# Row maxima of the attention layer: penalties subtracted on TensorE, a plain maximum over two units at a time on VectorE

## The chip, the cores and the metric

The kernel runs on one core of a Trainium2 chip. The metric is the device time of one execution of the whole program, in microseconds (us). The trace is that of one profiled execution.

## What is computed

The program runs four graph layers over 12500 nodes and 200000 edges, each followed by a layer normalisation. The change lies in the last one, an attention layer over the edges taken in both directions and a loop at every node:

```python
src = jnp.concatenate([src0, dst0, loop])
dst = jnp.concatenate([dst0, src0, loop])
xt = x @ W
s_node = xt @ a_src
d_node = xt @ a_dst
e_all = jnp.concatenate([e_contrib, e_contrib, zeros])
logits = leaky_relu(s_node[src] + d_node[dst] + e_all, 0.2)
m = segment_max(logits, dst)
z = exp(logits - m[dst])
out = segment_sum((z / segment_sum(z, dst)[dst])[:, None] * xt[src], dst)
```

The stage that the change touches finds, for each node, the largest `s_node[src] + e_all` over its edges (`d_node[dst]` is the same for all edges of a node and the leaky relu keeps the order, so both are put on afterwards).

## The kernel before

Edges lie in slots: a **group** `g` is 128 chunks (one per partition) of four edges (`SLOTS`), all of a group's edges ending in the same block of 128 nodes. There are 544 groups for each of the two directions `k`. A **unit** is one group of one direction: 128 × 4 = 512 edges. `QUAD` = 4 groups of both directions are handled together, so a **quad** is eight units, and there are 136 quads. The loop `skewed` runs `RING` = 4 quads to an iteration, 34 iterations, and lets stages run a quad or two ahead of one another.

The stage is the function `attention_maxima`. What each engine does for a quad:

- SyncE (`load`, L2007 and L2011) fetches the rows of direction 1 and, for both directions, the edges' node keys, broadcast to all partitions (512 KB each). The rows wait for the scores of two quads before, the keys for the penalties of two quads before.
- GpSimd (`gather`, L2046) fetches the rows of direction 0 with four indirect DMAs, and (`split`, L2032 to L2038) splits the 32 scores of each partition into three bf16 parts.
- VectorE (`scores`, L2114 and L2115) makes those scores, two quads ahead of the maxima.
- TensorE (`turn`, L2089) transposes the parts to `gT` (96 × 128), one quad ahead, and (`spread`, L2098) writes, for each unit, its 512 scores into all 128 partitions of one PSUM bank `wide[v]`, with four matmuls of 128 columns. The stationary operand `pick` selects one row of each part; nothing is accumulated.
- ScalarE (`copy_turned` L2078, `keep` L2065, `penalties` L2072) copies `gT` out of PSUM, keeps the scores, and makes for each direction `pen` = |key − partition| · 2^100 over 2048 edges: zero where the edge ends in the node of that partition, huge elsewhere.
- VectorE (`maxima`, L2127) makes, for each unit, one fused instruction that subtracts `pen` from `wide` and takes the maximum into one column of `gm`, followed by the read of its accumulator; then eight small maxima (L2136) of those columns into the blocks' entries of `tops`. At the head of each loop iteration it loads the iteration's block numbers into registers (`blocks`, L2140).

The order around the change is set by counted semaphores. TensorE's unit `e` may be written when the unit that last lay in its bank has been reduced; there are four banks, so TensorE runs up to four units ahead:

```python
wait(pe, s_max, q * 2 * QUAD + k * QUAD + v - QUAD + 1)
for r in range(SLOTS):
    m = nc.tensor.matmul(wide[v][:, r, :], pick[...], gT[:, u % 2, :], start=True, stop=True)
```

VectorE waits for `s_pen` (ScalarE's penalties) and `s_w` (TensorE's unit); ScalarE's penalties of quad `q` wait for `s_max` of quad `q - 2`, whose `pen` they overwrite.

Of the kernel before, what the change touches and what calls it, by code (L numbers as in the profile page):

```python
# [5 lines left out]
F32 = mybir.dt.float32  # L6
BF16 = mybir.dt.bfloat16
ALU = mybir.AluOpType
ACT = mybir.ActivationFunctionType
AX = mybir.AxisListType  # L10
# [4 lines left out]
P = 128  # L15
# [4 lines left out]
SLOTS = 4  # L20
# [723 lines left out]
def finished(*added):  # L744

    for s, n in added:
        s.base += n


def wait(eng, s, value):  # L750

    if isinstance(value, int) and value <= 0:
        return
    if isinstance(s, Count):
        eng.wait_ge(s.sem, value + s.base)
    else:
        eng.wait_ge(s, value)
# [1207 lines left out]

QUAD = 4
AHEAD = 3
FAR = 2.0 ** 100


def attention_maxima(nc, counts, D, K, name, XB, YB, score, tops):
# [6 lines left out]
    with ExitStack() as ctx:  # L1978
        def sb(nm, s, d=F32):
            return ctx.enter_context(nc.sbuf_tensor(f"{name}_{nm}", s, d))  # L1980
        keys = [sb(f"keys{k}", [P, 2, QUAD, SLOTS * P], BF16) for k in range(2)]
        pen = [sb(f"pen{k}", [P, 2, QUAD, SLOTS * P], BF16) for k in range(2)]
# [3 lines left out]
        gp = sb("gp", [P, 2, 3, NQ], BF16)  # L1986
        gT = sb("gT", [3 * NQ, 2, P], BF16)
        pick = sb("pick", [3 * NQ, NQ, P], BF16)
        junk = sb("junk", [P, 2, SLOTS * P], BF16)
        gm = sb("gm", [P, 2, 2 * QUAD])  # L1990
        far = sb("far", [P, 1])
        tp = [ctx.enter_context(nc.psum_tensor(f"{name}_t{u}", [3 * NQ, P], BF16)) for u in range(2)]
        wide = [ctx.enter_context(nc.psum_tensor(f"{name}_wide{u}", [P, SLOTS, P], F32)) for u in range(QUAD)]
        s_key = [[counts.get(f"expand_keys_loaded{k}{u}") for u in range(2)] for k in range(2)]
        s_in = [[counts.get(f"sum_rows_in{k}{u}", k == 0) for u in range(2)] for k in range(2)]
        s_pick, s_far = counts.get("top_pickers"), counts.get("top_far")
# [3 lines left out]
        with nc.Block() as block:  # L2000
            @block.sync
            def _(sp):
                def load(i, u):
                    q = i * RING + u
                    w = u % 2
                    wait(sp, s_g, q - 1)
                    sp.dma_start(rows[1][:, w, :, :, :].rearrange("p v r c -> p v (r c)"), view[:, bass.ds(q * QUAD, QUAD), :]).then_inc(s_in[1][w].sem, 16)  # L2007
                    for k, kr in enumerate((K.krA, K.krB)):
                        at = kr[0:1, 0:1]
                        wait(sp, s_pen, 2 * (q - 1))  # L2010
                        sp.dma_start(keys[k][:, w, :, :].rearrange("p v e -> p (v e)"),  # L2011
                                     bass.AP(tensor=at.tensor, offset=at.offset + q * (QUAD * SLOTS * P), ap=[[0, P], [1, QUAD * SLOTS * P]])).then_inc(s_key[k][w].sem, 16)
                skewed(sp, n, [(1, load)])
# [42 lines left out]

            @block.scalar
            def _(act):
                nc.scalar.activation(far[:, :], K.iotac[:, :], ACT.Copy, scale=-FAR).then_inc(s_far.sem, 1)
                wait(act, s_far, 1)  # L2060

                def keep(i, u):
                    q = i * RING + u
                    wait(act, s_g, q + 1)
                    nc.scalar.copy(score[:, :, bass.ds(q * QUAD, QUAD), :], g4[:, u % 2, :, :, :]).then_inc(s_kept.sem, 1)  # L2065

                def penalties(i, u):
                    q = i * RING + u
                    for k in range(2):
                        wait(act, s_key[k][u % 2], (i * (RING // 2) + u // 2 + 1) * 16)  # L2070
                        wait(act, s_max, (q - 1) * 2 * QUAD)
                        nc.scalar.activation(pen[k][:, u % 2, :, :], keys[k][:, u % 2, :, :], ACT.Abs, bias=far[:, :], scale=FAR).then_inc(s_pen.sem, 1)  # L2072

                def copy_turned(i, u):
                    q = i * RING + u
                    wait(act, s_t, q + 1)
                    wait(act, s_w, (q - 1) * 2 * QUAD)
                    nc.scalar.copy(gT[:, u % 2, :], tp[u % 2][:, :]).then_inc(s_tc.sem, 1)  # L2078
                skewed(act, n, [(1, copy_turned), (1, keep), (1, penalties)])

            @block.tensor
            def _(pe):
                wait(pe, s_pick, 6)

                def turn(i, u):
                    q = i * RING + u
                    wait(pe, s_gp, q + 1)
                    wait(pe, s_tc, q - 1)
                    nc.tensor.transpose(tp[u % 2][:, :], gp[:, u % 2, :, :].rearrange("p a e -> p (a e)"), K.identb[:, :]).then_inc(s_t.sem, 1)  # L2089

                def spread(i, u):
                    q = i * RING + u
                    wait(pe, s_tc, q + 1)
                    for k in range(2):
                        for v in range(QUAD):
                            wait(pe, s_max, q * 2 * QUAD + k * QUAD + v - QUAD + 1)
                            for r in range(SLOTS):
                                m = nc.tensor.matmul(wide[v][:, r, :], pick[:, (k * QUAD + v) * SLOTS + r, :], gT[:, u % 2, :], start=True, stop=True)  # L2098
                            m.then_inc(s_w.sem, 1)
                skewed(pe, n, [(1, turn), (0, spread)])  # L2100

            @block.vector
            def _(dve):
                held = {}

                def scores(i, u):
                    q = i * RING + u
                    w = u % 2
                    for k in range(2):
                        need = (i * (RING // 2) + u // 2 + 1) * 16  # L2110
                        wait(dve, s_in[k][w], need * QUAD if k == 0 else need)
                    wait(dve, s_kept, q - 1)
                    wait(dve, s_gp, q - 1)
                    nc.vector.tensor_tensor(g4[:, w, 0, :, :], rows[0][:, w, :, :, C], K.ecA[:, bass.ds(q * QUAD, QUAD), :], ALU.add)  # L2114
                    nc.vector.tensor_copy(g4[:, w, 1, :, :], rows[1][:, w, :, :, C]).then_inc(s_g.sem, 1)  # L2115

                def maxima(i, u):
                    q = i * RING + u
                    w = u % 2
                    for k in range(2):  # L2120
                        wait(dve, s_pen, 2 * q + k + 1)
                        for v in range(QUAD):
                            e = k * QUAD + v
                            wait(dve, s_w, q * 2 * QUAD + e + 1)
                            wait(dve, s_max, q * 2 * QUAD + e - 1)
                            dve.nop(nofuse=True)
                            nc.vector.tensor_tensor_reduce(out=junk[:, e % 2, :], in0=wide[v][:, :, :].rearrange("p r e -> p (r e)"),  # L2127
                                                           in1=pen[k][:, w, v, :], scale=1.0, scalar=-FAR, op0=ALU.subtract, op1=ALU.max,
                                                           accum_out=gm[:, w, e:e + 1]).then_inc(s_max.sem, 1)
                    wait(dve, s_max, (q + 1) * 2 * QUAD)  # L2130
                    for v in range(QUAD):
                        for k in range(2):
                            b = held[k][u * QUAD + v]
                            top, e = tops[2 * (v % 2) + k], k * QUAD + v
                            wait(dve, s_top, q * 2 * QUAD + 2 * v + k - 3)
                            nc.vector.tensor_tensor(top[:, bass.ds(b, 1)], top[:, bass.ds(b, 1)], gm[:, w, e:e + 1], ALU.max).then_inc(s_top.sem, 1)  # L2136

                def blocks(i):
                    for k in range(2):
                        held[k] = nc.values_load_multi_w_load_instructions(K.cblk[0:1, k, bass.ds(i * RING * QUAD, RING * QUAD)], engines=DVE_ONLY,  # L2140
                                                                           min_val=0, max_val=D.blocks - 1, skip_runtime_bounds_check_because=CLAMPED)[1]
                skewed(dve, n, [(2, scores), (0, maxima)], blocks)
        NQs = D.NG // QUAD
        for k in range(2):
            finished(*[(s, 8 * NQs) for s in s_key[k]], *[(s, (QUAD if k == 0 else 1) * 8 * NQs) for s in s_in[k]])
        finished((s_pick, 6), (s_far, 1), (s_g, NQs), (s_kept, NQs), (s_gp, NQs), (s_t, NQs), (s_tc, NQs), (s_pen, 2 * NQs),
                 (s_w, 2 * D.NG), (s_max, 2 * D.NG), (s_top, 2 * D.NG), (s_r, 3 * NQs))


def attention_sums(nc, counts, D, K, name, XB, YB, score, M3, accT):  # L2150
# [585 lines left out]
```

## Time and profile before

| | us |
|---|---|
| median of 3 runs | 16084.6 (16077.82 to 16091.67) |
| the profiled execution | 16079.79 |
| its span in the trace | 16078.1 |
| first fused maximum (L2127) starts | 13492.8 |
| last fused maximum (L2127) starts | 14563.0 |

The first two rows are device times; the span is that of the trace, and 1.7 us of the profiled execution lie outside of it. The two last rows bound the stage that the change touches: 1070.2 us, or 6.7% of the span. Over the whole span TensorE is busy 64% and VectorE 63%.

### The profile page before, as it was taken

The numbers are of one execution on the slowest core, as the hardware profiler recorded it, in microseconds if no ns is written. First come the engines' busy times: TensorE is split into PE (matmuls) and PEld (weight loads), VectorE is DVE, ScalarE is ACT, GpSimd is POOL, SyncE is SP. The second block draws the span as 40 slices with busy tenths as digits, with TensorE's granted clock in tenths as the row PEclk, the third lists the DMA queues.
The fourth block names the chain that finished last, engine by engine and source line by source line (L and its number), as shares of the span: only waits on it lengthen the run. The fifth ranks groups of instructions, "written<-read, shape, count | busy, mean of one in ns | idle before, by whom it ended". The sixth has DMA issues, their size and how long they took to land. (4 is left out here: it accounts for less than half of the span.)

```text
span 16078.1 us, 333902 instructions
## 1 busy us (share of the span) xinstructions
PE 10302.2 (64%) x72558; PEld 7980.5 (50%) x72559; DVE 10167.2 (63%) x36116; ACT 4495.2 (28%) x11901; POOL 9058.1 (56%) x10038
## 2 busy tenths in 40 slices
PE   6555555555537777767965656645566776667886
PEld 5333333333326666656853444422344664336886
DVE  9666666666643444437856777752365666887887
ACT  0111111111102333322113430025301223556886
POOL 0477777777745777767764445546400555554442
PEclk9777777777766777765556667755555665557998
DMA  9722222222242444453319997756653897885665
GB/s 369 303 80 79 81 81 79 79 83 79 79 94 58 80 80 80 80 79 71 68 28 279 324 309 223 224 163 218 191 176 89 279 278 257 270 267 204 212 212 160
DMA packets 2144346, 2589.93 MB, mean 161 GB/s; under 512 B 892242, under 2 KB 1761819, under 8 KB 2144195
## 3 DMA queue, kind: packets, MB, share of 16 engines
q1 hardware_dynamic: 1749158, 1741.66, 37.6%
q0 software_dynamic: 353792, 655.17, 13.1%
q10 hardware_dynamic: 41244, 191.56, 3.1%
q14 instruction: 115, 0.93, 0.0%
q8 instruction: 37, 0.61, 0.0%
HBM read 1738.44 MB, written 848.86 MB: 161 GB/s over the span
## 5 line engine op out<-in xcount | busy, mean ns | idle before, releaser
L566 POOL DMA_INDIRECT edges_by_dst<-rec,pos x1568 | 1541.2, 983 | 1029.1 <-DVE rec L501 555.5
L989 POOL DMA_INDIRECT sc_rows<-src_table,sc_idx x1664 | 1589.1, 955 | 607.9 <-issue 497.6
L566 POOL DMA_INDIRECT edges_by_cell<-rec,pos x1568 | 1545.5, 986 | 514.8 <-issue 497.4
L1756 PE MATMUL ex_rows<-table,ex_oh 128*128 x6528 | 1132.6, 339 | 884.8 <-DVE ex_stage L1732 335.7
L1844 PE MATMUL gs_part<-gs_rows,gs_oh 128*128 128x192 bf16 x6528 | 1024.4, 321 | 602.0 <-DVE gs_oh L1817 518.5
L1756 PEld LDWEIGHTS ex_rows<-table,ex_oh 128*128 128x128 bf16 x6528 | 724.9, 129 | 1292.3 <-issue 1252.6
L642 PE MATMUL xps<-ident,ea 128*128 128x128 f32 x784 | 216.4, 431 | 1740.9 <-DMA ea<-in_edge_attr_dram 1740.9
L1844 PEld LDWEIGHTS gs_part<-gs_rows,gs_oh 128*128 128x128 bf16 x6528 | 697.0, 131 | 929.3 <-issue 613.5
L2224 ACT ACTIVATE key_in_block<-at_rows,first_node 128x66 f32<-128x66 f32 x4352 | 1083.3, 336 | 266.2 <-PE at_part L2252 244.9
L2252 PE MATMUL at_part<-cell_edge_term,key_in_block 128*66 128x128 f32 x8704 | 1062.7, 286 | 115.3 <-issue 96.4
L530 DVE SCALAR_TENSOR_TENSOR junk<-rowb,keycol,earlier 128x128 f32<-128x128 f32 (+1 forms) x3136 | 1124.5, 415 | 1.8
L1724 DVE TENSOR_SCALAR ex_oh<-ex_keys,iotac 128x512 bf16<-128x512 bf16 x1632 | 568.2, 359 | 840.4 <-PE ex_rows L1756 628.1
L2252 PEld LDWEIGHTS at_part<-cell_edge_term,key_in_block 128*66 128x66 f32 x8704 | 1020.1, 146 | 137.4 <-issue 125.7
L642 PEld LDWEIGHTS xps<-ident,ea 128*128 128x128 f32 x784 | 139.5, 216 | 1818.7 <-issue 1818.6
L2204 POOL DMA_INDIRECT at_rows<-scored_rows_by_src,chunk_read_by_src x544 | 564.3, 1037 | 801.8 <-ACT key_in_block L2224 664.5
L635 PE MATMUL look<-Csb,ohT 128*128 128x256 f32 x3136 | 974.4, 441 | 0.7 <-DVE junk L543 0.7
L1951 PE MATMUL ex_rows<-table,ex_oh 128*128 x13056 | 783.9, 227 | 263.8 <-DVE own_terms L1924 144.3
L2098 PE MATMUL mx_wide<-mx_gT,mx_pick 96*128 96x128 bf16 x4352 | 653.9, 307 | 411.3 <-DVE mx_gm L2127 408.5
L1707 POOL DMA_INDIRECT dst_rows_by_src<-ex_stage,chunk_by_src x544 | 527.0, 969 | 632.7 <-DVE ex_stage L1732 508.6
L592 ACT COPY eaT<-xps 128x512 f32<-128x512 f32 x196 | 114.9, 586 | 2714.0 <-PE xps L642 2714.0
L1951 PEld LDWEIGHTS ex_rows<-table,ex_oh 128*128 128x128 bf16 x13056 | 700.5, 118 | 347.2 <-issue 307.3
L520 DVE TENSOR_TENSOR prod<-ea,a 128x128 f32<-128x128 f32 x196 | 58.1, 296 | 1280.1 <-DMA ea<-in_edge_attr_dram 1280.1
(402 smaller groups left out, 27327.5 us busy)
## 6 DMA issues: line engine op xcount, KB each, us to landing
ex_keys<-src_key_rows SPq DMA_DIRECT2D x1632, 128.0 KB
gs_rows<-dst_rows_by_src SPq DMA_DIRECT2D x1088, 192.0 KB
rowb<-sort_key_rows SPq DMA_DIRECT2D x392, 512.0 KB, 5.2
ex_keys<-dst_key_rows SPq DMA_DIRECT2D x1088, 128.0 KB
dst_rows_by_src<-patY ACTq DMA_DIRECT2D x1, 104448.0 KB, 417.2
rows_by_src<-ex_stage SPq DMA_DIRECT2D x544, 192.0 KB
scored_dst_rows_by_src<-patZ ACTq DMA_DIRECT2D x1, 71808.0 KB, 637.9
scored_rows_by_src<-ex_stage SPq DMA_DIRECT2D x544, 132.0 KB
```

The costliest lines, as they stand in the source:

```text
L530: nc.vector.scalar_tensor_tensor(junk[:, j % 4, k, 1 - odd:2, :], rowb[:, u, k, j - odd:j + 1, :], keycol[:, u, 1 - k, j:j + 1], earlier[: ...
L566: nc.gpsimd.indirect_dma_start(out=out, out_offset=bass.IndirectOffsetOnAxis(ap=pos[:, u, k, j:j + 1], axis=0), in_=row, in_offset=None).t ...
L635: m = nc.tensor.matmul(look[(u * PAIRS + c) % LOOKS][:, j % 2, :, :], ohT[:, u, j, :], Csb[:, c % 4, :, :], start=True, stop=True)
L989: nc.gpsimd.indirect_dma_start(out=rows[:, u, j, :], out_offset=None, in_=tabS, in_offset=bass.IndirectOffsetOnAxis(ap=idx[:, u, j:j + 1], ...
L1724: nc.vector.tensor_scalar(oh[k][:, u % 2, :], keys[k][:, u, :], K.iotac[:, :], None, ALU.is_equal).then_inc(s_oh[k].sem, 1)
L1756: m = nc.tensor.matmul(rows[k][u % 2][r // 2][:, r % 2, 0:W], oh[k][:, u % 2, r * P:(r + 1) * P], t3[:, bass.ds(held[k][u], 1), :].rearran ...
L1844: m = nc.tensor.matmul(part[k][u][:, 0, :], oh[k][:, u % 2, :, r], rows[k][:, u, r, :], start=r == 0, stop=r == SLOTS - 1)
L1951: m = nc.tensor.matmul(rows[k][u % 2][:, r, :], oh[k][:, u % 2, r * P:(r + 1) * P], t3[:, bass.ds(held[k][u], 1), part * W:(part + 1) * W] ...
L2098: m = nc.tensor.matmul(wide[v][:, r, :], pick[:, (k * QUAD + v) * SLOTS + r, :], gT[:, u % 2, :], start=True, stop=True)
L2204: nc.gpsimd.indirect_dma_start(out=rows[0][:, q % 2, v, :, :].rearrange("p r c -> p (r c)"), out_offset=None, in_=XB, in_offset=bass.Indir ...
L2224: m = nc.scalar.activation(msg[:, e % RING, r, :], rows[k][:, u % 2, v, r, :], ACT.Copy, scale=z[:, u % 2, k, v, r:r + 1])
L2252: m = nc.tensor.matmul(part[e % RING][:, 0, :], msg[:, e % RING, r, :], oh[:, e % RING, r, :], start=r == 0, stop=r == SLOTS - 1)
```

## The change

The subtraction moves from VectorE to TensorE. ScalarE makes once a constant `minus`, the negated identity (bf16). For each unit TensorE first multiplies it with that unit's 512 penalties, which writes their negative into the bank (`start=True`), and the four matmuls of `spread` now accumulate onto that (`start=False`). What lies in PSUM is then score minus penalty, and VectorE needs only a plain `tensor_reduce` with the maximum. It takes two units (two banks, 1024 elements, two results) at a time. The four banks are now two buffers of two banks (`WIDE` = 2) in place of four of one. `junk` goes away.

The waits follow. TensorE waits for the penalties (`s_pen`) itself, and for the reduction of the pair before last. ScalarE's penalties wait for TensorE's `s_w` in place of VectorE's `s_max`. `s_w` and `s_max` count pairs.

```diff
+WIDE = 2
...
-        junk = sb("junk", [P, 2, SLOTS * P], BF16)
+        minus = sb("minus", [P, P], BF16)
...
-        wide = [ctx.enter_context(nc.psum_tensor(f"{name}_wide{u}", [P, SLOTS, P], F32)) for u in range(QUAD)]
+        wide = [ctx.enter_context(nc.psum_tensor(f"{name}_wide{u}", [P, 2, SLOTS, P], F32)) for u in range(WIDE)]
...
+                nc.scalar.activation(minus[:, :], K.identb[:, :], ACT.Copy, scale=-1.0).then_inc(s_far.sem, 1)
                 nc.scalar.activation(far[:, :], K.iotac[:, :], ACT.Copy, scale=-FAR).then_inc(s_far.sem, 1)
-                wait(act, s_far, 1)
+                wait(act, s_far, 2)
...
-                        wait(act, s_max, (q - 1) * 2 * QUAD)
+                        wait(act, s_w, (q - 1) * QUAD)
                         nc.scalar.activation(pen[k][:, u % 2, :, :], keys[k][:, u % 2, :, :], ACT.Abs, bias=far[:, :], scale=FAR).then_inc(s_pen.sem, 1)
...
-                    wait(act, s_w, (q - 1) * 2 * QUAD)
+                    wait(act, s_w, (q - 1) * QUAD)
...
                     for k in range(2):
-                        for v in range(QUAD):
-                            wait(pe, s_max, q * 2 * QUAD + k * QUAD + v - QUAD + 1)
-                            for r in range(SLOTS):
-                                m = nc.tensor.matmul(wide[v][:, r, :], pick[:, (k * QUAD + v) * SLOTS + r, :], gT[:, u % 2, :], start=True, stop=True)
+                        wait(pe, s_pen, 2 * q + k + 1)
+                        for h in range(QUAD // 2):
+                            e = k * (QUAD // 2) + h
+                            wait(pe, s_max, q * QUAD + e - WIDE + 1)
+                            for v in (2 * h, 2 * h + 1):
+                                to = wide[e % WIDE][:, v % 2, :, :]
+                                nc.tensor.matmul(to.rearrange("p r e -> p (r e)"), minus[:, :], pen[k][:, u % 2, v, :], start=True, stop=False)
+                                for r in range(SLOTS):
+                                    m = nc.tensor.matmul(to[:, r, :], pick[:, (k * QUAD + v) * SLOTS + r, :], gT[:, u % 2, :],
+                                                         start=False, stop=r == SLOTS - 1)
                             m.then_inc(s_w.sem, 1)
...
-                    for k in range(2):
-                        wait(dve, s_pen, 2 * q + k + 1)
-                        for v in range(QUAD):
-                            e = k * QUAD + v
-                            wait(dve, s_w, q * 2 * QUAD + e + 1)
-                            wait(dve, s_max, q * 2 * QUAD + e - 1)
-                            dve.nop(nofuse=True)
-                            nc.vector.tensor_tensor_reduce(out=junk[:, e % 2, :], in0=wide[v][:, :, :].rearrange("p r e -> p (r e)"),
-                                                           in1=pen[k][:, w, v, :], scale=1.0, scalar=-FAR, op0=ALU.subtract, op1=ALU.max,
-                                                           accum_out=gm[:, w, e:e + 1]).then_inc(s_max.sem, 1)
-                    wait(dve, s_max, (q + 1) * 2 * QUAD)
+                    for e in range(QUAD):
+                        wait(dve, s_w, q * QUAD + e + 1)
+                        dve.nop(nofuse=True)
+                        nc.vector.tensor_reduce(gm[:, w, 2 * e:2 * e + 2], wide[e % WIDE][:, :, :, :].rearrange("p v r e -> p v (r e)"),
+                                                AX.X, ALU.max).then_inc(s_max.sem, 1)
+                    wait(dve, s_max, (q + 1) * QUAD)
```

How this stands on the two engines, in the first loop iteration. On VectorE the eight fused maxima of a quad, each with the read of its accumulator, stand before the eight small maxima; of those 16 rows the first six:

```order
L2127 ISA mx_junk,mx_gm<-mx_wide,mx_pen 128x512
L2127 ISA mx_gm 128x1
L2127 ISA mx_junk,mx_gm<-mx_wide,mx_pen 128x512
L2127 ISA mx_gm 128x1
L2127 ISA mx_junk,mx_gm<-mx_wide,mx_pen 128x512
L2127 ISA mx_gm 128x1
```

In their place the changed kernel has, for a whole quad, between the scores and the small maxima:

```order
L2123 TENSOR_TENSOR mx_g<-mx_rows,cell_edge_term 128x16
L2124 COPY mx_g<-mx_rows 128x16
L2132 TENSOR_REDUCE mx_gm<-mx_wide 128x2 x4
L2140 ISA
L2140 TENSOR_TENSOR tops<-tops,mx_gm 128x1
```

Sixteen instructions became four.

On TensorE a quad was a transpose and 32 matmuls of 128 columns:

```order
L2089 MATMUL mx_t<-identb,mx_gp 96x128
L2098 MATMUL mx_wide<-mx_gT,mx_pick 128x128 x32
```

In the changed kernel it is the same with a matmul of 512 columns ahead of each four, eight times in a quad; its first two pairs of units:

```order
L2092 MATMUL mx_t<-identb,mx_gp 96x128
L2104 MATMUL mx_wide<-mx_pen,mx_minus 128x512
L2106 MATMUL mx_wide<-mx_gT,mx_pick 128x128 x4
L2104 MATMUL mx_wide<-mx_pen,mx_minus 128x512
L2106 MATMUL mx_wide<-mx_gT,mx_pick 128x128 x4
L2104 MATMUL mx_wide<-mx_pen,mx_minus 128x512
L2106 MATMUL mx_wide<-mx_gT,mx_pick 128x128 x4
L2104 MATMUL mx_wide<-mx_pen,mx_minus 128x512
L2106 MATMUL mx_wide<-mx_gT,mx_pick 128x128 x4
```

The columns that TensorE streams for a unit went from 512 to 1024, and they stand in one queue with no other work between.

## Rows read from the trace of the kernel before

**Rows 1.** Busy time by stretch: the changed stage, then three stages with bf16 or fp32 matmuls.

```profile
core 0: us, PE busy (x) PEld busy (x) DVE busy (x) ACT busy (x) POOL busy (x), PEclk, DMA share, GB/s
13493.00:14563.00 1070.00, 659.23 (x4470) 394.50 (x4470) 872.52 (x3519) 578.16 (x537) 626.09 (x1066) 0.50 0.81 265
12450.00:13400.00 950.00, 715.98 (x11924) 639.27 (x11920) 586.05 (x2489) 218.82 (x994) 482.57 (x498) 0.69 0.90 279
9700.00:10500.00 800.00, 514.48 (x3637) 379.40 (x3636) 596.30 (x1816) 0.00 (x0) 455.27 (x455) 0.78 0.74 224
14600.00:15900.00 1300.00, 1153.83 (x12373) 1106.21 (x12374) 1093.12 (x2577) 1044.04 (x4260) 527.40 (x513) 0.93 0.62 212
```

**Rows 2.** Groups of instructions in the stage: busy us, mean ns, idle before and releaser.

```profile
L2127 DVE CUSTOM_DVE_ANT_0 mx_junk<-mx_wide,mx_pen 128x512 bf16<-128x512 f32 x1088 | 675.8, 687 | 25.0 <-ACT mx_pen L2072 18.2 <-issue 6.2
L2098 PE MATMUL mx_wide<-mx_gT,mx_pick 96*128 96x128 bf16 x4352 | 653.9, 307 | 411.3 <-DVE mx_gm L2127 408.5
L2072 ACT ACTIVATE mx_pen<-mx_keys,mx_far 128x2048 bf16<-128x2048 bf16 x272 | 529.5, 1994 | 158.1 <-DVE mx_gm L2127 158.1
L2136 DVE TENSOR_TENSOR tops<-tops,mx_gm 128x1 f32 x1088 | 161.7, 160 | 38.4 <-DVE mx_gm L2127 28.7 <-DVE tops L2136 0.3
```

**Rows 3.** Who waited for whom in the stage: us in total, times, longest us.

```profile
PEld mx_wide L2098 <- DVE mx_gm L2127: 650.5, 911, 5.6
POOL mx_gp L2032 <- DVE mx_g L2115: 207.4, 122, 5.5
DVE mx_g L2114 <- issue: 134.1, 129, 3.3
```

**Rows 4.** Instructions in order of time, one quad from 13999.43 to the next.

```profile
13999.43 0.69 DVE L2127 CUSTOM_DVE_ANT_0 mx_junk<-mx_wide,mx_pen 128x512 bf16<-128x512 f32 x1 [0.20 <-issue]
14000.05 0.08 DVE L2127 DVE_READ_ACCUMULATOR2_ANT mx_gm<- 128x1 f32 x1
14000.05 0.69 DVE L2127 CUSTOM_DVE_ANT_0 mx_junk<-mx_wide,mx_pen 128x512 bf16<-128x512 f32 x1
...
14000.66 0.08 DVE L2127 DVE_READ_ACCUMULATOR2_ANT mx_gm<- 128x1 f32 x1
14000.66 0.69 DVE L2127 CUSTOM_DVE_ANT_0 mx_junk<-mx_wide,mx_pen 128x512 bf16<-128x512 f32 x1
14000.80 0.34 PEld L2098 LDWEIGHTS mx_wide<-mx_gT,mx_pick 96*128 96x128 bf16 x4 [0.27 <-DVE mx_gm L2127]
...
14002.42 0.31 PE L2089 MATMUL mx_t<-identb,mx_gp 128*96 128x128 bf16 x1
...
14002.87 0.26 ACT L2078 COPY mx_gT<-mx_t 96x128 bf16<-96x128 bf16 x1 [4.58 <-PE mx_t L2089]
...
14004.33 0.08 DVE L2127 DVE_READ_ACCUMULATOR2_ANT mx_gm<- 128x1 f32 x1
...
14004.63 1.26 DVE L2136 TENSOR_TENSOR tops<-tops,mx_gm 128x1 f32 x8 [0.22 <-DVE mx_gm L2127]
...
14006.13 0.18 DVE L2114 TENSOR_TENSOR mx_g<-mx_rows,cell_edge_term 128x16 f32<-128x16 f32 x1 [0.24 <-issue]
...
14006.56 0.69 DVE L2127 CUSTOM_DVE_ANT_0 mx_junk<-mx_wide,mx_pen 128x512 bf16<-128x512 f32 x1 [0.16 <-ACT mx_pen L2072]
```

**Rows 5.** The same view at the loop's head: VectorE's stop while it loads block numbers.

```profile
14030.75 0.18 DVE L2114 TENSOR_TENSOR mx_g<-mx_rows,cell_edge_term 128x16 f32<-128x16 f32 x1 [3.22 <-issue]
```

**Rows 6.** The same view at the stage's start: 16 spread matmuls with nothing to wait for.

```profile
13489.44 1.91 PE L2098 MATMUL mx_wide<-mx_gT,mx_pick 96*128 96x128 bf16 x16
```

**Rows 7.** Groups of the whole span: TENSOR_REDUCE on VectorE at three sizes.

```profile
L1103 DVE TENSOR_REDUCE scores<-sc_qk 128x256 f32 x408 | 168.3, 412 | 0.0
L1290 DVE TENSOR_REDUCE sm_edge<-sm_pen 128x1 f32<-128x1664 f32 x2 | 3.8, 1886 | 0.1
L884 DVE TENSOR_REDUCE ln_m<-x_nodes 128x104 f32<-128x6656 f32 x4 | 28.3, 7086 | 1.7 <-PEq L2421 1.1 <-PEq L788 0.6
```

**Rows 8.** The only bf16 matmul of 512 columns in the trace.

```profile
L614 PE MATMUL xps<-zero 128*128 128x512 bf16 x1 | 0.6, 586 | 2.9 <-PEq L352 2.9
```

More of the change, by code:

```diff
@@ L2083, in _ @@
                 wait(pe, s_pick, 6)
+                wait(pe, s_far, 2)
                 def turn(i, u):
@@ L2145, in attention_maxima @@
             finished(*[(s, 8 * NQs) for s in s_key[k]], *[(s, (QUAD if k == 0 else 1) * 8 * NQs) for s in s_in[k]])
-        finished((s_pick, 6), (s_far, 1), (s_g, NQs), (s_kept, NQs), (s_gp, NQs), (s_t, NQs), (s_tc, NQs), (s_pen, 2 * NQs),
-                 (s_w, 2 * D.NG), (s_max, 2 * D.NG), (s_top, 2 * D.NG), (s_r, 3 * NQs))
+        finished((s_pick, 6), (s_far, 2), (s_g, NQs), (s_kept, NQs), (s_gp, NQs), (s_t, NQs), (s_tc, NQs), (s_pen, 2 * NQs),
+                 (s_w, D.NG), (s_max, D.NG), (s_top, 2 * D.NG), (s_r, 3 * NQs))
 def attention_sums(nc, counts, D, K, name, XB, YB, score, M3, accT):
```

## The prediction

> **What bounds the stage now.** I read the busy time by stretch first [rows 1]. In the changed stage VectorE is busy 872 of 1070 us, TensorE 659, ScalarE 578, GpSimd 626, the DMA engines 0.81. Nothing is full, so the waits decide. They say [rows 3] that TensorE waits for VectorE's maxima (650 us), GpSimd for VectorE's scores (207 us), and VectorE for "issue", its own registers and branches (134 us). VectorE is the pace. The order of time shows a quad in full [rows 4]: the fused maxima start 0.61 us apart (13999.43, 14000.05, 14000.66), the last accumulator read ends at 14004.41, 4.98 us after the start, then come 0.22 us, eight small maxima (1.26 us), 0.24 us, the scores, and the next quad at 14006.56. A quad is **7.13 us: 4.98 us of maxima and 2.15 us of tail.** Every fourth quad has a stop of 3.22 us in place of 0.24 [rows 5]; 136 × 7.13 + 34 × 2.98 = 1071 us, the stage's 1070. TensorE hides: it needs about 0.43 us for a unit against VectorE's 0.61, and four banks let it run ahead. Its clock was granted at 0.50 throughout (1.2 GHz) [rows 1].
>
> **VectorE's part.** Eight fused maxima go, four TENSOR_REDUCE of 1024 elements come. The rows for that operation [rows 7] are 412 ns at 256, 1886 ns at 1664, 7086 ns at 6656, thus 1.042 ns an element and 0.15 us fixed; 1024 elements give 1886 − 640 × 1.042 = **1.22 us**. The fused one lasts 0.687 us and starts every 0.612 [rows 2, 4], so 0.075 us of it overlaps the next; I give the reduce the same, a pitch of **1.144 us**. If VectorE alone decided, a quad's maxima would last 3 × 1.144 + 1.22 = 4.65 us in place of 4.98: 0.33 us less, 45 us over 136 quads. That is all there is to gain; two fused units cost 1.225 us, one pair 1.144. The Trainium skill (VectorE: DVE Perf Modes, "The DRAIN you can't avoid") speaks against even that: it says that the next operation does not start until the pipe is empty, and grants an earlier start only to one that isn't held. By its first half the reduces would start 1.22 us apart, and the sum below, in its full-rate quads, would be some 6 us higher; the fused rows overlap, so I keep 1.144.
>
> **TensorE's part.** Sixteen matmuls back to back took 1.91 us [rows 6]; less one matmul's length beyond its pitch (0.314 − 0.107) that is 0.107 us per 128 columns at 1.2 GHz. The added matmul has 512 columns, so 0.427 us. The one such row of the trace [rows 8] is 586 ns long against 314 for 128 columns, 0.27 more for 384 columns, which would make it 0.38; I take 0.427, since back-to-back pitch is what counts here. Weight loads overlap, as they do now. A pair of units costs 2 × (0.427 + 4 × 0.107) = **1.71 us at half rate**, half of that, **0.85 us, at full rate** (2.4 GHz). A quad needs 6.8 us or 3.4 us of TensorE.
>
> **The hand-over is the point.** There are now two buffers, each a pair. TensorE may fill a buffer only when its reduce is over, and VectorE may read only when it is full. From [rows 4]: accumulator read over at 14000.74, weight load at 14000.80, so 0.06 us that way; transpose over at 14002.73, ScalarE's copy at 14002.87, so 0.14 us the other way. Let a quad's first reduce start at 0 with both buffers full (TensorE had the 2.15 us tail for that).
>
> - Half rate: reduce 0 ends at 1.22, TensorE fills from 1.28 to 2.99, its last matmul's result is there at 3.20, reduce 2 starts at 3.34 instead of 2.29. The second fill follows directly: its result at 4.91, reduce 3 starts at 5.05 and ends at 6.27. Against 4.98 now: **+1.29 us**, with a quad of 8.42 us, of which TensorE works 6.9.
> - Full rate (the same 0.21 us beyond the pitch): reduce 2 starts at 2.48; the other buffer is free at 2.42, reduce 3 starts at 3.62 and ends at 4.84: **−0.14 us**.
>
> So all quads at half rate would give +175 us, all at full rate −19 us.
>
> **Which rate.** The stage now streams 512 columns a unit in short bursts and is granted 0.50. It will stream 1024, at half rate nearly without a break inside a quad. The stages in which TensorE works in long bursts with stops are granted 0.69 and 0.78, the one that hardly stops 0.93 [rows 1]. Here a full-rate quad leaves TensorE idle for half of it, and each iteration has the stop of [rows 5], so I take the stretches with stops as the nearest: full rate 0.38 and 0.56 of the time, half rate 0.62 and 0.44. I put **half of the quads at half rate**: 0.5 × 1.29 − 0.5 × 0.14 = 0.575 us a quad, × 136 = **+78 us**; the two ends, 0.44 and 0.62, give +67 and +102.
>
> **The rest at nothing.** ScalarE's penalties (2 × 1.99 us [rows 2]) now start when TensorE has read those of two quads before, earlier in the cycle than now; with the two copies ScalarE has 4.5 us of work in a quad of 7 or more. TensorE's new wait for them should find them done: they start when the spread of the quad before starts, and are over after about 4.5 us of its 7. If that cover went, the spread would wait for them, and behind it in TensorE's queue the transpose of the next quad. The key loads wait for the penalties of two quads before, as now, and have over 8 us. The DMA engines and GpSimd (0.81 and 626 us of 1070) get more time, not less. Making `minus` is one 128-column ScalarE instruction, under 0.5 us once. The small maxima and the loop's stop stay.
>
> **Sum:** 16079.8 (the profiled execution) + 78 = 16158; the median of the runs lies 4.8 us above that execution, so **16163 us**, 0.5% slower. A difference under 0.2% (32 us) cannot be told from none here.
>
> **Rivals.**
>
> - *Half rate throughout* (0.12). The clock stays at 0.50 because TensorE stops about 1.5 us in each quad and longer at the loop's head. For it: 0.50 in 1070 us now. Against it: in every stage with longer bursts it rose. 16085 + 175 = 16260.
> - *Full rate throughout* (0.10). Work doubles, the clock rises and stays, and the hand-over nearly vanishes: −19 us, 16066. For it: 0.93 in the last stretch. Against it: that stretch keeps TensorE 89% busy, this would be near half at that rate. The Trainium skill (TensorE: Matmul & The Clock Gate, Part 1) says that the throttled state is the default and sustained activity lifts it, which leans this way; its part on a second failure mode says that brief idle times while PSUM banks are cycled make the clock oscillate, which leans to my forecast.
> - *The other side: VectorE never waits* (0.07). If a fill with both hand-overs takes no more than one reduce (1.07 us from the end of reduce 0 to 2.29), the four reduces run at their pitch: 4.65 us, −45 us, 16040. It decides at a fill of about 0.7 us a pair; full rate gives 0.85, or 0.79 with the shorter matmul of [rows 8]. It needs full rate and a shorter latency at once.
> - *The change doesn't relieve VectorE*: the reduce over two banks has no row here. At 1.22 us pitch nothing is gained, +6 us on the sum; that lies in my range.
>
> **Numbers.** My case has 0.71, its own range 16146 to 16190 from the two clock shares. The range for 8 in 10 reaches up to the half-rate case and down a little beyond my case, to 16100: 16100 to 16262 leaves out the two fast rivals. Faster by over 0.2% (under 16052): 0.08. Within 0.2% (16052 to 16117): 0.14. Slower: 0.78.
>
> **What would show it.** TENSOR_REDUCE near 1.22 us, its third in a quad waiting on the spread (L2106): about 1 us in half-rate quads, 0.2 in full-rate ones. The granted clock of the stage 0.65 to 0.8, quads of about 8.4 and 7.0 us in turns, and the stage near 1150 us. TensorE's wait for VectorE shrinks from 650 us. I am wrong if VectorE waits for penalties or scores instead, if the clock stays at one level, or if the quads at half rate are no longer than now.

## The result, and the profile after

The changed kernel takes **16210.2 us** (median of 4 runs, 16204.9 to 16217.9) against 16081.2 for the kernel before (4 runs). The ratio is 1.0081, with a 95% interval of 1.0069 to 1.0093: 129 us slower. The forecast was 16163 us with a range of 16100 to 16262.

The extra time lies in the changed stage. From the first to the last start of the large maxima it took 1070.2 us before (13492.8 to 14563.0) and now takes 1200.1 us (13500.6 to 14700.7). The other 8 us by which the profiled spans differ (16216.2 against 16078.1) passed ahead of the stage, in code that is unchanged.

The busy time of the stage (the window starts 8 us ahead of its first maximum and ends 11 us ahead of its last), with the same two other stretches as in [rows 1] (columns as there):

```profile
13493.00:14690.00 1197.00, 767.71 (x5507) 503.42 (x5508) 839.57 (x1870) 574.12 (x541) 631.87 (x1075) 0.75 0.71 238
12450.00:13400.00 950.00, 712.49 (x11901) 636.79 (x11897) 581.63 (x2482) 218.21 (x992) 481.06 (x496) 0.69 0.90 278
9700.00:10500.00 800.00, 517.96 (x3636) 382.56 (x3637) 596.93 (x1818) 0.00 (x0) 455.74 (x454) 0.77 0.74 223
```

VectorE's busy share fell from 872 of 1070 us to 840 of 1197, TensorE's time grew from 659 to 768 us, and its granted clock rose from 0.50 to 0.75. The stage is slower although the work moved to an engine that had room and now runs at a higher rate on average. So VectorE, which sets the pace, must wait more. The groups of the stage show for what:

```profile
L2132 DVE TENSOR_REDUCE mx_gm<-mx_wide 128x2 f32<-128x1024 f32 x544 | 652.8, 1222 | 136.0 <-PE mx_wide L2106 132.4
L2104 PE MATMUL mx_wide<-mx_pen,mx_minus 128*128 128x512 bf16 x1088 | 565.5, 520 | 428.6 <-DVE mx_gm L2132 424.3 <-ACT mx_gT L2080 0.7
L2106 PE MATMUL mx_wide<-mx_gT,mx_pick 96*128 96x128 bf16 x4352 | 559.5, 267 | 0.0
L2074 ACT ACTIVATE mx_pen<-mx_keys,mx_far 128x2048 bf16<-128x2048 bf16 x272 | 529.6, 1994 | 0.0
L2140 DVE TENSOR_TENSOR tops<-tops,mx_gm 128x1 f32 x1088 | 171.4, 160 | 80.0 <-DVE mx_gm L2132 31.9 <-DVE tops L2140 5.6
```

A reduce of a pair lasts 1.222 us. VectorE stood idle before the reduces for 136.0 us, 132.4 of them for the spread (L2106); in [rows 2] the fused maxima had 25.0 us, none for TensorE. ScalarE's penalties no longer wait for VectorE. There is a second line that I had not looked for: idle time before the small maxima doubled, from 38.4 to 80.0 us, and only 31.9 of it is a wait for the reduce.

One quad in order of time, VectorE alone; it answers to [rows 4]:

```profile
13999.87 1.22 DVE L2132 TENSOR_REDUCE mx_gm<-mx_wide 128x2 f32<-128x1024 f32 x1
14002.01 1.23 DVE L2132 TENSOR_REDUCE mx_gm<-mx_wide 128x2 f32<-128x1024 f32 x1 [0.92 <-PE mx_wide L2106]
14003.53 1.22 DVE L2132 TENSOR_REDUCE mx_gm<-mx_wide 128x2 f32<-128x1024 f32 x1 [0.30 <-PE mx_wide L2106]
```

The first row is the quad's second reduce. The third starts 2.14 us after it, 0.92 us of them idle; the fourth is late by another 0.30. Both wait for TensorE, as the hand-over would have it. TensorE over the same time:

```profile
14000.01 0.61 PE L2104 MATMUL mx_wide<-mx_pen,mx_minus 128*128 128x512 bf16 x1 [5.47 <-DVE mx_gm L2132]
14000.41 0.63 PE L2106 MATMUL mx_wide<-mx_gT,mx_pick 96*128 96x128 bf16 x4
...
14000.84 0.63 PE L2104 MATMUL mx_wide<-mx_pen,mx_minus 128*128 128x512 bf16 x1
...
14003.32 0.38 PE L2104 MATMUL mx_wide<-mx_pen,mx_minus 128*128 128x512 bf16 x1
...
14008.35 0.39 PE L2104 MATMUL mx_wide<-mx_pen,mx_minus 128*128 128x512 bf16 x1 [2.47 <-DVE mx_gm L2132]
```

The refill starts at 14000.01 after 5.47 us of idling (this is the quad behind the loop's head, where VectorE loads its block numbers). Units start 0.83 us apart (14000.01, 14000.84). From 14003.32 on, the same matmul lasts 0.38 us in place of 0.61. And after that TensorE stands idle 2.47 us again. The granted clock of three stretches of this quad (columns as in [rows 1]) makes the order plain:

```profile
14000.00:14002.20 2.20, 2.19 (x12) 1.36 (x13) 1.28 (x2) 0.00 (x0) 1.44 (x2) 0.50 1.02 388
14002.20:14004.60 2.40, 2.17 (x21) 1.48 (x19) 2.10 (x2) 1.00 (x3) 1.79 (x3) 0.81 0.56 180
14004.60:14008.30 3.70, 1.06 (x10) 0.65 (x10) 2.87 (x13) 3.25 (x2) 1.47 (x5) 1.00 0.26 73
```

The refills that VectorE waits for run at 0.50 nearly to their end. The clock has risen to 1.00 when only the two pairs of the next quad are left, for which VectorE has time, and when TensorE then idles.

The next quad shows another order. Its refills, from 14008.35 on, start at full rate in spite of the 2.47 us of idling, and the clock falls while TensorE works on them; the fourth reduce is late again:

```profile
14008.35:14009.48 1.13, 1.06 (x11) 0.65 (x11) 1.07 (x1) 0.00 (x0) 0.70 (x1) 1.00 0.34 123
14009.48:14011.00 1.52, 1.52 (x12) 1.12 (x13) 1.23 (x1) 0.00 (x0) 1.21 (x2) 0.65 0.89 256
14011.09 1.23 DVE L2132 TENSOR_REDUCE mx_gm<-mx_wide 128x2 f32<-128x1024 f32 x1 [0.35 <-PE mx_wide L2106]
```

Over all 136 quads of this trace, the mean granted clock while TensorE fills the first, second, third and fourth pair of a quad is 0.68, 0.90, 0.70 and 0.57. VectorE waits for the last two. Behind the loop's head all 34 third pairs start at 0.50; of the other 102, 32 do and 70 start at 1.00. A mean of 0.75 over the stage hides that the full rate comes in good part where nobody waits.

Over all 136 quads, from the starts in the two traces (means):

| part of a quad, us | before | after | difference | × 136 |
|---|---|---|---|---|
| first to last start of the large maxima | 4.284 | 4.576 | +0.292 | +40 |
| last of them to the first small maximum | 0.914 | 1.467 | +0.554 | +75 |
| first to last small maximum | 1.092 | 1.446 | +0.353 | +48 |
| last small maximum to the next quad (loop's heads included) | 1.61 | 1.36 | −0.24 | −33 |

The first two together are the large maxima: +115 us. The third is the unforeseen part. All of the last row's difference lies between the second score instruction and the first large maximum (0.36 us before, 0.11 after): the fused maximum waited there for the penalties too, which alone was 18.2 us of idle time [rows 2].

### The profile page after: what moved, and what is told of

It reads as the page before. It is cut to its first block and busy times, and to the rows that moved or that the text cites. A ratio compares the mean times of both kernels' runs of the same rounds, so it can differ in the third digit from the quotient of the medians.

```text
span 16216.2 us, 332553 instructions
## 1 busy us (share of the span) xinstructions
PE 10429.8 (64%) x73646; PEld 8101.7 (50%) x73647; DVE 10143.0 (63%) x34484; ACT 4487.8 (28%) x11902; POOL 9057.3 (56%) x10038
## 5 line engine op out<-in xcount | busy, mean ns | idle before, releaser
L2104 PE MATMUL mx_wide<-mx_pen,mx_minus 128*128 128x512 bf16 x1088 | 565.5, 520 | 428.6 <-DVE mx_gm L2132 424.3
```

The lines of the kernel that those rows point to most:

```text
L2104: nc.tensor.matmul(to.rearrange("p r e -> p (r e)"), minus[:, :], pen[k][:, u % 2, v, :], start=True, stop=False)
```

## The experiments

They ran on chips on which the kernel before takes 18553 to 18762 us. That extra time lies in other stages: the changed stage is as long there (1074.7 us before the change, 1205.5 us after it, by the traces of the two repeats below). So the runs are compared by their ratio to the kernel before on the same chip, and by the length of the stage. The 95% intervals of the ratios are 20 to 35 us wide to either side. The stage's length comes from one trace a run, often of another chip; where a kernel was traced twice, it came out within 6 us (1070.2 and 1074.7, 1200.1 and 1205.5, 999.0 and 999.1). The two measures can differ: for the first four experiments, and for single units with two waits, the ratio puts the kernel 24 to 33 us lower against the kernel before than the stage does (1074.7 us taken for the kernel before). "Stage" is always from the first to the last start of the large maxima; the times that an expectation gives for the whole kernel refer to the first runs (16081 and 16210 us), and their differences carry over.

**Both kernels again.**

> The kernel before again, for its trace on the chip of the experiments. All theories: no difference; from first to last fused maximum of a quad 4.28 us, the small maxima 1.09 us, and the stage 1070 to 1090 us.

> The changed kernel again, beside the experiments. All theories: slower than the kernel before by the same 120 to 140 us in absolute terms; from first to last reduce of a quad 4.5 to 4.65 us, the small maxima 1.45 us.

Before: ratio 0.9994 (0.9983 to 1.0004), stage 1074.7 us, 4.283 us from first to last, small maxima 1.092. Changed: 18682 us, ratio 1.0076 (1.0057 to 1.0095), stage 1205.5 us, 4.60 and 1.446 us. The change costs the same 130 us here.

**No penalties on TensorE.**

```diff
-nc.tensor.matmul(to.rearrange("p r e -> p (r e)"), minus[:, :], pen[k][:, u % 2, v, :], start=True, stop=False)
...
-                                                         start=False, stop=r == SLOTS - 1)
+                                                         start=True, stop=True)
```

> The changed kernel without the 512-column matmul of the penalties; the four spread matmuls write the bank directly, and everything else (pairs, two buffers, plain reduce, waits) stays. What it leaves out: the penalties, so the maxima run over all edges of a group. Theory A (VectorE waits for TensorE's refill of the buffers): the third and fourth reduce of a quad start 1.14 us after the one before, from first to last 3.4 us in place of 4.58, and 136 x 1.15 = 156 us go: 16050 to 16060. Rival B (the reduces or their waits are slow by themselves, or the register work of VectorE's tail sets the pace): the gaps stay above 1.3 us and the time above 16150.

Ratio 0.9995 (0.9983 to 1.0007), stage 1092.2 us: 113 us less than the changed kernel's. VectorE's idle time before the reduces (with its releasers) and the stage's clock:

```profile
L2131 DVE TENSOR_REDUCE mx_gm<-mx_wide 128x2 f32<-128x1024 f32 x544 | 641.3, 1220 | 28.6 <-issue 9.4 <-DMA sm_scores_dram<-sm_turn 9.3
15831.00:16924.00 1093.00, 574.51 (x4470) 438.99 (x4470) 840.74 (x1892) 571.67 (x537) 626.72 (x1066) 0.50 0.78 260
```

The wait for the spread is nearly gone, with the same reduces, buffers and waits: theory A holds, and B falls. (The wait goes with a fill of 0.85 us in place of 1.71, so this run doesn't tell the amount of work from its rate.) But not all 156 us went. Without the added columns the clock stayed at 0.50, so a pair's fill was 8 × 0.107 = 0.85 us, the figure of my full-rate case, and the third reduce came 1.28 us after the second; the hand-over sum of the prediction gives 2.48 − 1.14 = 1.34 for such a fill. The reduces still spanned 3.58 us, not 3.42. And from the last small maximum to the next quad two quads of four took 0.36 and 0.41 us longer than in the changed kernel. What held these up isn't settled; the traces name mostly "issue" there.

**More work, to raise the clock.**

```diff
+        spare = ctx.enter_context(nc.psum_tensor(f"{name}_spare", [P, SLOTS * P], F32))
...
+                            for _ in range(4 if e == WIDE else 0):
+                                nc.tensor.matmul(spare[:, :], minus[:, :], pen[k - 1][:, u % 2, 0, :], start=True, stop=True)
                             wait(pe, s_max, q * QUAD + e - WIDE + 1)
```

> The changed kernel with four useless matmuls of 512 columns a quad, into a spare PSUM bank, put where TensorE stands idle: after the second pair, ahead of its wait for VectorE. Theory E (what costs is that the refills which VectorE waits for run at half rate, and more TensorE work before them raises the granted clock there): the granted clock of the stage rises from 0.75 to over 0.85, the fourth reduce starts nearer to 1.2 us after the third than 1.65, and the time falls by 50 to 110 us. Rival F (TensorE's amount of work decides, at whatever rate): 4 x 0.427 us more, of which 0.2 us or more a quad are not hidden: 20 to 60 us more.

Ratio 1.0025 (1.0013 to 1.0036), stage 1146.1 us, 59 us less than the changed kernel's 1205.5. The stage's row:

```profile
15836.00:16984.00 1148.00, 769.33 (x5973) 469.58 (x6104) 848.18 (x1892) 572.08 (x538) 626.73 (x1067) 0.89 0.74 247
L2135 DVE TENSOR_REDUCE mx_gm<-mx_wide 128x2 f32<-128x1024 f32 x544 | 650.1, 1221 | 74.4 <-PE mx_wide L2109 35.3 <-issue 22.9 <-DMA sm_scores_dram<-sm_turn 6.0
```

TensorE was given four useless matmuls of 512 columns a quad, 25% more columns, and the kernel became faster. The clock went from 0.75 to 0.89, the third reduce followed after 1.41 us instead of 1.81 and the fourth after 1.51 instead of 1.65. By the ratios the gain is larger, about 95 us (1.0025 against 1.0076). This is what tells theory E from F: not the amount of work, but the rate at which the refills run.

**Finer units.**

```diff
-wide = [... nc.psum_tensor(f"{name}_wide{u}", [P, 2, SLOTS, P], F32) for u in range(WIDE)]
+wide = [... nc.psum_tensor(f"{name}_wide{u}", [P, SLOTS, P], F32) for u in range(QUAD)]
...
-wait(pe, s_max, q * QUAD + e - WIDE + 1)
+wait(pe, s_max, q * 2 * QUAD + e - QUAD + 1)
...
-nc.vector.tensor_reduce(gm[:, w, 2 * e:2 * e + 2], wide[e % WIDE][...], AX.X, ALU.max)
+nc.vector.tensor_reduce(gm[:, w, e:e + 1], wide[e % QUAD][...], AX.X, ALU.max)
```

> The penalties stay on TensorE, but four buffers of one bank as before the change, and VectorE reduces one unit (512 elements) at a time. TensorE streams the same columns. Theory A (two buffers of pairs are too coarse a hand-over): at half rate the last unit of a quad is late by about 0.2 us, at full rate none; from first to last reduce 4.3 to 4.5 us, the wait from the last reduce to the small maxima 0.55 us shorter, the register additions gone with the pairs' counts; 16060 to 16090, about the time before the change. Rival G (the doubled columns of TensorE cost in themselves, however handed over): above 16150.

Ratio 1.0003 (0.9991 to 1.0014), stage 1112.9 us. From first to last reduce 4.32 us, 0.905 to the small maxima: as expected. TensorE streams as many columns as in the changed kernel, and the 130 us are down to 38. G falls: by the table's first two parts the doubled columns cost next to nothing when the hand-over is fine enough (4.32 and 0.905 us against 4.284 and 0.914 before the change). One part of the expectation failed: the small maxima still took 1.448 us, though the counts were no longer in pairs.

```profile
16402.46 4.29 DVE L2132 TENSOR_REDUCE mx_gm<-mx_wide 128x1 f32<-128x512 f32 x7
16407.03 0.69 DVE L2132 TENSOR_REDUCE mx_gm<-mx_wide 128x1 f32<-128x512 f32 x1 [0.28 <-PE mx_wide L2106]
16407.94 1.61 DVE L2140 TENSOR_TENSOR tops<-tops,mx_gm 128x1 f32 x8 [0.23 <-issue]
```

Seven reduces without a stop, 0.28 us of waiting at the eighth, about as expected; then 1.61 us for the eight small maxima, 1.26 in [rows 4].

**Two waits at the small maxima.** The order of instructions in the loop shows what the prediction missed. Each small maximum waits on the counter `s_top` with a value that depends on the loop index, so it must stand in a register. Before the change six of eight such waits found their value made already, by additions that stood between the fused maxima and ran under them:

```
L2136 ISA
L2136 TENSOR_TENSOR tops<-tops,mx_gm 128x1
L755 REGISTER_ALU
L2136 ISA
L2136 TENSOR_TENSOR tops<-tops,mx_gm 128x1
L2136 ISA
L2136 TENSOR_TENSOR tops<-tops,mx_gm 128x1
L2136 ISA
```

In the changed kernel an addition stands ahead of six of the seven that follow the first:

```
L2140 ISA
L2140 TENSOR_TENSOR tops<-tops,mx_gm 128x1
L755 REGISTER_ALU
L2140 ISA
L2140 TENSOR_TENSOR tops<-tops,mx_gm 128x1
L755 REGISTER_ALU
L2140 ISA
L2140 TENSOR_TENSOR tops<-tops,mx_gm 128x1
```

The traces have a small maximum with the addition 0.217 us after the one before, without it 0.145. Five more of them are 5 × 0.072 = 0.36 us a quad; the table has 0.353.

The count in pairs, which the expectation for single units blames, is not what took the values away: with single units the additions stand in the same places, and the small maxima take the same time. What both kernels lack is the wait of each fused maximum on VectorE's own count, which went with `junk`:

```python
wait(dve, s_max, q * 2 * QUAD + e - 1)
wait(dve, s_top, q * 2 * QUAD + 2 * v + k - 3)
```

The first line's values for the first six units are those that the second line needs at the third to the eighth small maximum, and in the kernel before these six waits read the same registers.

The experiment waits only before the first and the fifth:

```diff
-                            wait(dve, s_top, q * 2 * QUAD + 2 * v + k - 3)
+                            if k == 0 and v % 2 == 0:
+                                wait(dve, s_top, q * 2 * QUAD + 2 * v)
```

> The changed kernel, in which the eight small maxima of a quad wait on their own counter twice instead of eight times. Theory C (in the changed kernel each of those waits needs a register addition of its own, since its value is no longer one that another wait has made): the small maxima span about 1.05 us from first to last start instead of 1.45, 136 x 0.4 = 54 us less: about 16155 to 16170. Rival D (a shorter tail of VectorE is eaten by a longer wait for TensorE at the next quad): no more than 15 us less.

Ratio 1.0025 (1.0010 to 1.0040), stage 1154.6 us, 51 us less than the changed kernel's. The small maxima span 1.095 us instead of 1.446 (48 us). The row of the group, against 80.0 us of idle time in the changed kernel:

```profile
L2141 DVE TENSOR_TENSOR tops<-tops,mx_gm 128x1 f32 x1088 | 151.3, 160 | 50.8 <-issue 15.7 <-DVE mx_gm L2132 15.1
```

C holds; D, that TensorE's lateness would eat it, does not: at two buffers TensorE has time in VectorE's tail. The edit doesn't weigh the additions alone, though: it takes out six waits with them, and the fifth small maximum now starts 0.298 us after the fourth where the others take 0.129 to 0.141. That the sum comes to 0.35 again is partly luck. The counterpart is the same edit in the kernel before:

> The kernel before, with two waits in place of eight at the small maxima and nothing else. Theory C (there the waits cost hardly anything, since their values were already in registers for other waits; only the first had an addition): the small maxima from 1.09 to 1.02 to 1.09 us, the stage 0 to 10 us shorter. Rival (the eight waits cost as much there, and the changed kernel's tail was long for another reason): 30 us or more shorter.

Ratio 1.0004 (0.9991 to 1.0016), stage 1080.1 us against 1074.7, small maxima 1.090 us in place of 1.092: nothing to gain there (the stage was to get 0 to 10 us shorter and came out 5 us longer, which is within the scatter). The eight waits were no dearer than two before, so the additions are a cost that the change brought. With single units, where the additions were still there:

> The kernel with single units (penalties on TensorE, four buffers of one bank, one unit a reduce) and two waits at the small maxima. Theory C (the register additions are what held it above the kernel before): the small maxima 1.10 us from first to last in place of 1.45, the stage 1113 - 48 = 1065 us, that of the kernel before, and the time within 0.1% of it. Rival: the tail's gain is eaten by TensorE at half rate, which is then late for the next quad: the stage stays above 1095.

Ratio 0.9992 (0.9980 to 1.0004), stage 1085.4 us. The small maxima fell to 1.086 us, but the stage only by 28 of 48 us, to 1085.4 where 1065 was expected: the last reduce of a quad now came 0.86 us after the one before in place of 0.71. Here the rival has a part: with VectorE's quad shorter, TensorE is late at its end.

**Three pair buffers.** TensorE gets six banks. The buffer of a pair is its number in the loop iteration modulo three; an iteration has 16 pairs, so at its head the wait is stricter.

```diff
-wide = [... [P, 2, SLOTS, P], F32) for u in range(WIDE)]
+wide = [... [P, 2, SLOTS, P], F32) for u in range(3)]
...
-                            wait(pe, s_max, q * QUAD + e - WIDE + 1)
+                            j = u * QUAD + e
+                            wait(pe, s_max, q * QUAD + e - (2 if j > 2 else 0 if j == 0 else 3))
...
-                                to = wide[e % WIDE][:, v % 2, :, :]
+                                to = wide[j % 3][:, v % 2, :, :]
...
-nc.vector.tensor_reduce(gm[:, w, 2 * e:2 * e + 2], wide[e % WIDE][...], AX.X, ALU.max)
+nc.vector.tensor_reduce(gm[:, w, 2 * e:2 * e + 2], wide[(u * QUAD + e) % 3][...], AX.X, ALU.max)
```

> The changed kernel with three pair buffers (six PSUM banks) in place of two. TensorE has the same work and the same rate to fear. Theory A (the hand-over over two coarse buffers makes VectorE wait for TensorE): from first to last reduce 3.45 to 3.7 us in place of 4.58; the stage 120 to 150 us shorter than the changed kernel's 1200, so about 10 us less to 20 us more than before the change, unless the fetches of the rows hold VectorE's scores back, as the run without penalties hints (its tails were 0.3 us longer in two quads of four), which gives back up to 40 us. Rival G (TensorE's doubled columns at half rate, 6.9 us a quad, set the pace whatever the buffers): at least 80 us of the 130 remain.

Ratio 0.9986 (0.9974 to 0.9997), stage 1045.9 us: 160 us less than the changed kernel on the same chip, and a little less than the kernel before. VectorE no longer waits:

```profile
L2133 DVE TENSOR_REDUCE mx_gm<-mx_wide 128x2 f32<-128x1024 f32 x544 | 628.1, 1216 | 4.3 <-DMA sm_scores_dram<-sm_turn 2.0 <-issue 1.4 <-PE mx_wide L2107 0.7
15674.00:16721.00 1047.00, 720.82 (x5558) 470.01 (x5556) 828.13 (x1892) 571.24 (x537) 626.38 (x1066) 0.80 0.82 271
16099.66 4.62 DVE L2133 TENSOR_REDUCE mx_gm<-mx_wide 128x2 f32<-128x1024 f32 x4
```

Four reduces take 4.62 us (the prediction's 4.65 with VectorE alone), the wait for the spread is 0.7 us in all, with the stage's mean clock hardly higher than in the changed kernel (0.80 against 0.75). That mean hides a rise where it counts: from the end of a quad's first reduce to the start of its fourth the clock is 0.82 on average, against 0.62 in the changed kernel. But the rise isn't what removes the wait. In 31 of the 136 quads the clock stands at 0.50 through that whole stretch, and there too no reduce starts more than 1.142 us after the one before. One of them:

```profile
15781.91:15784.09 2.18, 2.12 (x12) 1.40 (x13) 2.18 (x3) 0.00 (x0) 1.41 (x3) 0.50 0.99 226
15780.69 4.62 DVE L2133 TENSOR_REDUCE mx_gm<-mx_wide 128x2 f32<-128x1024 f32 x4
```

One more buffer is worth more than the clock. The same with the two waits:

> Three pair buffers, and two waits in place of eight at the small maxima. If both gains stand beside each other: 45 us less than with three buffers alone, 40 to 60 us less than the kernel before. If the quad, then at 6.6 to 6.9 us, meets TensorE's 6.9 us at half rate or the fetches of the rows, most of those 45 us are waited away again: 0 to 25 us less than the kernel before.

> Three pair buffers and two waits again, with more rounds: 0.3 to 0.6% less than the kernel before, the stage near 1000 us.

Ratio 0.9952 (0.9933 to 0.9970) and, again, 0.9955 (0.9939 to 0.9971): **0.45% faster than the kernel before** (18670 against 18755 us in the second), and it beats both kernels. The stage is 999.0 and 999.1 us, 76 less than before the change; both gains stand beside each other in full. Its busy time in the second run:

```profile
15852.00:16851.00 999.00, 684.30 (x5455) 458.99 (x5555) 807.43 (x1890) 571.49 (x537) 628.71 (x1066) 0.81 0.85 284
```

## Why the prediction was right, and where it was too low

The direction and the mechanism were right, and the time lies in the range; the difference was +129 us where +78 was worked out. By the steps of the prediction:

- **The reduce.** 1.22 us was forecast, 1.222 measured; the pitch 1.144 against 1.141. The rule of the Trainium skill that I had weighed (VectorE: DVE Perf Modes, "The DRAIN you can't avoid"), taken by its first half, does not hold here: reduces that wait for nothing start 0.08 us before the one before is over. Its second half, that an operation which isn't held starts earlier, agrees.
- **TensorE's fill.** Units 0.83 us apart at half rate against 0.85. Right.
- **The hand-over.** At half rate the third reduce was to start 2.20 us after the second (3.34 − 1.14) and the fourth 1.71 after the third; the medians of quads whose refills run wholly at half rate are 2.13 and 1.71. At full rate 1.34 was forecast for the third; 1.305 is the median of the 36 quads in which it waits at full rate only. The experiments with three buffers and with single units show that this is the cause.
- **The share of half-rate quads** is the term that was mis-sized. I took a half, from the share of time in stages that work in bursts. The stage's clock, 0.75 over all, is even at their level. But the two refills that VectorE waits for get the low rate far more often than the mean says. Read from the clock itself, it is 0.62 on average from the end of the first reduce to the start of the fourth, thus half rate for 75% of that time; measured by the spread of the reduces (4.576 us, between 4.98 at half and 3.59 at full rate) the share is 0.71. Against my mean of 4.33 for the same span, that is 0.24 us a quad, 33 us.
- **"The small maxima stay"**, costed at nothing, was wrong: +0.35 us a quad for register additions, and −0.24 us ahead of the next quad, where the waits for the penalties and for VectorE's own count are gone. Net 15 us. The wait before the small maxima was 0.03 us longer than taken, another 4 us. 78 + 33 + 15 + 4 = 130 us, the stage's growth.
- **At nothing:** key loads and `minus`, rightly. ScalarE's penalties cost nothing either, but they were a gain: VectorE had stood idle for them for 18.2 us in the kernel before [rows 2], and the sum carries that time on in its tail of 2.15 us.
- **Two slips in the working,** on which nothing hangs: the two clock shares give 16152 to 16187 where the prediction has 16146 to 16190, and a pair with the shorter matmul is 0.38 + 4 × 0.107 = 0.81 us at full rate, not 0.79.

Of the rivals, *half rate throughout* and *full rate throughout* fell with 0.75: both levels occur in most quads. *The change doesn't relieve VectorE* fell with the pitch of 1.141 us. *VectorE never waits* is what three buffers brought about, by their number and not by faster fills.

The Trainium skill (TensorE: Matmul & The Clock Gate, Part 1) says that sustained activity lifts the throttled default; the experiment with useless work agrees in direction (0.75 to 0.89). The Trainium skill (same page, "A second HAM failure mode") also says that brief idle times between groups of matmuls, while PSUM banks are cycled, make the clock go up and down; the stage agrees, its clock fell 127 times in 136 quads.

## What to carry to other kernels

Moving work from a busy engine to an idle one pays only if the buffers between them still cover the receiver's longer fill: here each step grew on both sides while the number of steps ahead fell from four to two, and one more buffer turned a loss of 0.8% into a gain of 0.1% (0.45% with the cheaper waits). When TensorE works in bursts that another engine paces, don't price the matmuls that are waited for at the stage's mean clock; here they ran at half rate for 75% of their time where the stage did for 50%, and the clock rose late and fell late. After dropping a wait or changing what a counter counts, look at the instruction order for new register additions ahead of the waits that are left, and give short instructions as few index-dependent waits as correctness needs.

## What the runs showed of the hardware

A useless load can be worth its time: 4 matmuls of 512 columns a quad, put into TensorE's idle time, raised the granted clock from 0.75 to 0.89 and shortened the stage by 59 us. The clock trails the work: behind idle times of 2 to 2.5 us TensorE still started 70 of 102 refills at full rate, and in the second refill of these 70 quads its clock was 0.62 on average. A register addition before a wait costs VectorE 0.072 us when nothing longer runs on the engine (0.217 against 0.145 us between small instructions), and nothing under a long one (the fused maxima start 0.611 us apart with one addition between them and with two). Left open is what lengthens the tail of some quads by up to 0.4 us in the runs whose quads are shorter than the changed kernel's, in the one without penalties above all.
